# Projecting the values of a gated delta mixer once and convolving them on VectorE, a chunk ahead

## The reference, cut to what matters

```
q = x @ w_q;  k = x @ w_k;  v = x @ w_v                 # 1024, 1024 and 2048 channels
beta = sigmoid(x @ w_b) * 2
g = -exp(A_log) * softplus(x @ w_a + dt_bias)
q, k, v = silu(conv4(q)), silu(conv4(k)), silu(conv4(v)) # causal, depthwise, 4 taps in time
q, k = l2norm(q), l2norm(k)
for t:                                                   # per head, S is 64 x 128
    S = S * exp(g_t);  mem = k_t @ S
    S = S + k_t^T (v_t - mem) * b_t;  o_t = (q_t / 8) @ S
y = o * rsqrt(mean(o*o) + eps) * norm_w * silu(x @ w_g)
out = y @ w_out
```

## Time and profile before

| | us |
|---|---|
| median of 3 runs | 5771.28 |
| profiled execution, own time | 5775.05 |
| its span, first to last instruction | 5773.2 |
| TensorE busy | 5136.3 (89%) |
| VectorE busy | 3784.4 (66%) |
| ScalarE busy | 2786.2 (48%) |
| GpSimd busy | 2260.3 (39%) |
| stretch of the 32 chunks of the first mixer | 69 to about 2965 |

### The profile page before, as it was taken

How to read it: one execution, slowest core, us unless ns; L and a number is a source line. 1 busy time by engine, 2 the same in 40 slices (tenths; PEclk the granted TensorE clock), 3 DMA queues, 4 the chain that set the end, 5 groups by cost and what they waited for, 6 DMA issues and landing times. The chain is left out here.

```text
span 5773.2 us, 105253 instructions
## 1 busy us (share of the span) xinstructions
PE 5136.3 (89%) x36890; PEld 3594.2 (62%) x36890; DVE 3784.4 (66%) x8870; ACT 2786.2 (48%) x6575; POOL 2260.3 (39%) x1588
## 2 busy tenths in 40 slices
PE   5999999999899999999989989995578787998998
PEld 3776776767677677776766646652146675664665
DVE  5656656566565665656658848845699736875884
ACT  1444444444344444444438838844400113883882
POOL 2424334243232433424337717713422114762761
PEclk7999999999999999999989989997699757998998
DMA  3000000000000000000010000000000000000000
GB/s 110 5 7 7 4 7 5 5 7 4 9 4 7 7 4 7 5 5 7 4 32 1 0 27 1 0 7 0 0 8 1 1 1 28 0 18 10 0 0 15
DMA packets 170268, 53.55 MB, mean 9 GB/s; under 512 B 142225, under 2 KB 166161, under 8 KB 169233
## 3 DMA queue, kind: packets, MB, share of 16 engines
q1 hardware_dynamic: 168736, 49.54, 3.7%
q10 hardware_dynamic: 1392, 2.20, 0.1%
HBM read 41.21 MB, written 10.49 MB: 9 GB/s over the span
## 5 line engine op out<-in xcount | busy, mean ns | idle before, releaser
L342 PE MATMUL gd_ps<-gd_taps,gd_xwin 128*128 128x512 f32 x2048 | 907.3, 598 | 8.0 <-ACT gd_qT L528 8.0
L342 PEld LDWEIGHTS gd_ps<-gd_taps,gd_xwin 128*128 128x128 f32 x2048 | 382.7, 191 | 465.5 <-issue 446.0
L787 POOL TENSOR_TENSOR gd_o_rn<-gd_tmp,gd_mhalf 128x8 f32<-128x8 f32 x64 | 103.5, 1635 | 1193.6 <-DVE gd_tmp L706 1193.6
L551 ACT ACTIVATE gd_X<-gd_ps 128x512 f32<-128x512 f32 x512 | 268.2, 633 | 541.6 <-PE gd_ps L384 541.6
L1298 ACT ACTIVATE L_ffn_s<-L_ffn_s,L_ffn_nb,L_ffn_r 128x128 f32<-128x128 f32 x1024 | 419.4, 482 | 3.1
L683 DVE TENSOR_TENSOR gd_Z<-gd_ps,cst 128x256 f32<-128x256 f32 x384 | 163.0, 425 | 327.0 <-PE gd_ps L422 261.0
L1118 POOL TENSOR_TENSOR L_ffn_t<-L_ffn_t 128x512 f32<-128x512 f32 x128 | 190.3, 1487 | 394.3 <-DVE L_ffn_t L1339 394.3
L781 POOL TENSOR_TENSOR gd_gate<-gd_gate,gd_norm_w 128x2048 f32<-128x2048 f32 x32 | 145.0, 4531 | 483.4 <-ACT gd_gate L516 483.4
L384 PE MATMUL gd_ps<-cst,gd_gV 128*128 128x128 f32 x2048 | 264.9, 278 | 53.8 <-DMA gd_gV<-gd_inverses 29.5
L384 PEld LDWEIGHTS gd_ps<-cst,gd_gV 128*128 128x128 f32 x2048 | 225.8, 143 | 77.5 <-ACT gd_decay L546 74.8
L516 ACT ACTIVATE gd_v<-gd_ps 128x512 f32<-128x512 f32 x128 | 76.4, 597 | 406.2 <-PE gd_ps L342 406.2
(11 more groups left out here) (376 smaller groups left out, 13405.1 us busy)
## 6 DMA issues: line engine op xcount, KB each, us to landing
L_ffn_sb_rope<-in_rope SPq DMA_DIRECT2D x4, 2048.0 KB, 8.2
gd_tap_row<-in_L_attn_conv_v SPq DMA_DIRECT2D x2, 2048.0 KB, 7.1
gd_blocks<-gd_nA SPq DMA_DIRECT2D x256, 16.0 KB, 1.7
gd_Z<-gd_blocks SPq DMA_DIRECT2D x32, 128.0 KB, 2.0
gd_inverses<-gd_Z SPq DMA_DIRECT2D x32, 128.0 KB, 1.7
gd_gV<-gd_inverses SPq DMA_DIRECT2D x256, 16.0 KB, 1.9
L_ffn_sb_wqkv<-in_L_ffn_wqkv SPq DMA_DIRECT2D x4, 768.0 KB, 8.7
gd_tap_row<-in_L_attn_conv_q SPq DMA_DIRECT2D x1, 2048.0 KB, 15.4
```

The costliest lines, as they stand in the source:

```text
L342: ins = pe.matmul(ps[4 + i % 2][:], xwin[:, t:t + P] if i < 8 else xwin[:, PAD:PAD + P], taps[:, t, 512 * SLICE[i]:512 * (SLICE[i] + 1)] i ...
L551: act.activation(heads(X, gi).rearrange("p h x -> p (h x)"), ps[4 + gi][:], ACT.Copy).then_inc(x_s.sem, 1)
```

## The change

For v the four tap-scaled copies of the weights go away. w_v and its taps are loaded as they are. Per chunk TensorE multiplies each of the 16 blocks of 128 value channels once with the whole window of 131 columns (`plain_values`), with channels on the partitions and time along the columns; three blocks share a PSUM bank, so there are six steps, through banks 4 and 5. ScalarE copies them to `plain_v`. VectorE convolves (`convolve`): for each of the 16 blocks one tensor_scalar for the first tap and three scalar_tensor_tensor that add the other taps, each on a window shifted by one column, 64 operations per chunk. TensorE then turns each result back (`pe.transpose`, four per `project` 4 to 7), and ScalarE evicts with Silu as before.

The plain values and the convolution of chunk n+1 are done within `late` of chunk n: the matmuls behind gate slice 11 and ahead of k·S, the 16 first-tap operations ahead of the levels, and two of the other 48 behind each mask and each addition. `xwin_v` is a second window, filled by GpSimd at the head of `late`. For the first chunk of a batch the plain values come ahead of `early` and all 64 operations stand between `norms_and_decays` and `mid`; the last chunk of a batch has nothing ahead.

```diff
-        taps = sb("taps", [P, TAPS, QKV])
+        taps = sb("taps", [P, TAPS, 2 * H * DK])
+        w_v = sb("w_v", [P, H * DV])
+        taps_v = sb("taps_v", [P, H, TAPS])
...
-            conv_src = [W["conv_q"], W["conv_k"], W["conv_v"][0:1024], W["conv_v"][1024:2048]]
+            conv_src = [W["conv_q"], W["conv_k"]]
...
+                    act.dma_start(w_v[:], W["w_v"]).then_inc(weights_in, 16)
+                    act.dma_start(taps_v[:], W["conv_v"].rearrange("(m p) t -> p m t", p=P)).then_inc(weights_in, 16)
...
-                    for q in range(4):
-                        dve.wait_ge(taps_in[q % 2], 16 * (q // 2 + 1))
+                    for q in range(2):
+                        dve.wait_ge(taps_in[q], 16)
...
+                    elif i < 8:
+                        if i == 4:
+                            w(cv_s.now(n))
+                        for k in range(4):
+                            ins = pe.transpose(out[:, P * k:P * (k + 1)], conv_v[:, 4 * (i - 4) + k], ident)
...
+                def plain_values(n, i):
+                    if i == 0:
+                        w(win_v.now(n))
+                    if i >= 2:
+                        w(pv_out.now(n, i - 2))
+                    for j in range(min(VPER, H - VPER * i)):
+                        m = VPER * i + j
+                        ins = pe.matmul(ps[4 + i % 2][:, (PAD + P) * j:(PAD + P) * (j + 1)], w_v[:, DV * m:DV * (m + 1)], xwin_v[:], start=True, stop=True)
+                    ins.then_inc(pv_mm.sem, 1)
...
                     for i in range(5, 12):
                         project(n, i)
+                    if ahead:
+                        for i in range(VSTEPS):
+                            if i < 2:
+                                w(proj_out.now(n, 10 + i))
+                            plain_values(n + 1, i)
...
                         if g0 == 0:
-                            w(proj_out.now(n, 11))
+                            w(pv_out.now(n + 1) if ahead else proj_out.now(n, 11))
...
+                    for i in range(VSTEPS):
+                        plain_values(b * NC, i)
+                    w(pv_out.now(b * NC))
                     early(b * NC)
...
+                def convolve(n, first, count):
+                    for j in range(first, first + count):
+                        t, m = divmod(j, H)
+                        window, tap = plain_v[:, m, t:t + P], taps_v[:, m, t:t + 1]
+                        if t:
+                            w(cv_s.now(n, j - H))
+                            ins = dve.scalar_tensor_tensor(conv_v[:, m], window, tap, conv_v[:, m], ALU.mult, ALU.add)
+                        else:
+                            if m % VPER == 0:
+                                w(pv_out.now(n, m // VPER))
+                            ins = dve.tensor_scalar(conv_v[:, m], window, tap, None, ALU.mult)
+                        ins.then_inc(cv_s.sem, 1)
...
+                    if ahead:
+                        convolve(n + 1, 0, H)
...
                             dve.tensor_tensor(heads(Z, gi), ps[gi][:, 0:256].rearrange("p (h x) -> p h x", h=HG), mask, ALU.mult).then_inc(z_s.sem, 1)
+                            if ahead:
+                                convolve(n + 1, H + 16 * l + 2 * gi, 2)
...
+                            if ahead:
+                                convolve(n + 1, H + 16 * l + 8 + 2 * gi, 2)
...
                     norms_and_decays(b * NC)
+                    convolve(b * NC, 0, TAPS * H)
                     mid(b * NC)
```

More of the change, by code:

```diff
@@ L113 @@
 DECAY_FLOOR = -1.0e4
+VPER = 3
+VSTEPS = -(-H // VPER)
 def load_and_transpose(nc, A, cst, xT, sems):
@@ L206, in _ @@
                     dve.memset(mhalf[:], -0.5).then_inc(zeros, 1)
-                    dve.wait_ge(raw_in, 48)
-                    for q in range(4):
-                        dve.wait_ge(taps_in[q % 2], 16 * (q // 2 + 1))
+                    dve.wait_ge(raw_in, 32)
+                    for q in range(2):
+                        dve.wait_ge(taps_in[q], 16)
                         for t in range(TAPS):
@@ L253, in sig @@
             return Signal(sems("gd_" + name), per, primed)
-        win = sig("window", 1)
+        win, win_v = sig("window", 1), sig("window_v", 1)
+        pv_mm, pv_out, cv_s = sig("plain_v_mm", VSTEPS), sig("plain_v", VSTEPS), sig("conv_v", TAPS * H)
         ab_mm, ab_out = sig("ab_mm", 1), sig("ab_out", 1)
@@ L340, in project @@
                         w(t_out.now(n, i - 2))
[L341 to L344, removed]
-                    ins.then_inc(proj_mm.sem, 1)
+                    out = ps[4 + i % 2]
+                    if i < 4:
+                        for t in range(TAPS):
+                            ins = pe.matmul(out[:], xwin[:, t:t + P], taps[:, t, 512 * SLICE[i]:512 * (SLICE[i] + 1)],
+                                            start=(t == 0), stop=(t == TAPS - 1))
+                    elif i < 8:
[4 more added lines that the diff above has]
+                    else:
+                        ins = pe.matmul(out[:], xwin[:, PAD:PAD + P], w_g[:, 512 * (i - 8):512 * (i - 7)], start=True, stop=True)
+                    ins.then_inc(proj_mm.sem, 1)
+                def plain_values(n, i):
[7 more added lines that the diff above has]
+                    ins.then_inc(pv_mm.sem, 1)
                 def early(n):
@@ L516, in project, with plain_values @@
                     act.activation(dst, src, ACT.Silu).then_inc(proj_out.sem, 1)
+                def plain_values(n):
+                    for i in range(VSTEPS):
+                        w(pv_mm.now(n, i))
+                        m = min(VPER, H - VPER * i)
+                        act.activation(plain_v[:, VPER * i:VPER * i + m].rearrange("p m x -> p (m x)"), ps[4 + i % 2][:, 0:(PAD + P) * m],
+                                       ACT.Copy).then_inc(pv_out.sem, 1)
                 def early(n):
@@ L537, in mid, with late @@
                     copy_qk(n, 0)
-                def late(n):
+                def late(n, ahead):
                     for i in range(4, 12):
                         project(n, i)
+                    if ahead:
+                        w(cv_s.now(n))
+                        plain_values(n + 1)
                     for gi in range(G):
@@ L794, in _ @@
                         n = b * NC + c
+                        w(pv_mm.now(n))
+                        window_v(n + 1, b, c + 1)
                         late(n)
```

33 lines of the change are left out of this document (19 added, 14 removed).

## The result

| | before | after |
|---|---|---|
| median of the runs | 5772.8 us (5764.0 to 5775.0) | 6135.6 us (6125.0 to 6141.6) |
| the profiled execution, its span | 5775.05, 5773.2 | 6125.01, 6123.2 |
| granted TensorE clock, mean | 0.934 | 0.894 |

The changed kernel takes 1.063 times as long (95% interval 1.061 to 1.065). That is slower, as forecast, but 26 us beyond the upper end of the range of 5880 to 6110 and 96 us above the predicted 6040.

The account below looks back on a forecast made before the run. The chain from nA to the landed inverse, without TensorE, was taken as the bound. 30 chunks at +7.65 us (230), two last (7), starts +46 and set-up -13 gave +270: 6040 us predicted, range 5880 to 6110.

Parts of the forecast that it names:

- Part 1: TensorE between nA and the landed inverse: the 8.5 us saved per chunk become wait, except -0.75 us for q·S copies.
- Part 2: GpSimd's gate multiply, now earlier, stops VectorE's block inverse through the shared port: +4.4 us per chunk on the chain.
- The small reads of the earlier trace: GpSimd's 2.90 us power operation, reading 16 elements, let six chained VectorE operations pass undisturbed, 0.2 us each.
- Part 3: TensorE's longer idle before the turning of T drops its clock to 1.2 GHz: +1.7 us per chunk.
- The one case I priced it by: After a 5.23 us TensorE idle, 16 transposes took 3.98 us instead of 1.92; the clock was 1.00 in the stretch behind.
- Part 4: VectorE's convolution lengthens level 64: +2.3 us in each of 30 chunks; covered ahead of and in levels 16 and 32.
- Part 5: Batch starts and set-up: nA of a batch's first chunk 23 us later, twice, +46; set-up -13.
- PE busy less by about 240: A sign named in advance: TensorE's busy time falls by about 240 us while the mixer gets longer.
- (a): Rival: the port does not stop the inverse, since GpSimd waits or the gate is done before; 5900 us, chance 0.28.
- (b): Rival: the convolution lies on the path in full, 5.4 us for 2.3, with the port stop; 6135 us, chance 0.05.
- (c): Rival: same time, with inverse undisturbed, convolution hidden in TensorE's time and clock kept; 5780 us, chance 0.03.
- (d): Rival: faster, the inverse's landing follows TensorE's pace, so its 8.5 us per chunk come through; 5600 us, chance 0.04.

Follow-up runs that it names:

- b2: The kernel before with one tap of four for v and GpSimd's gate multiply made to wait for the block inverse's end; 5873 us, 1.018 times before.
- b1: The kernel before with one tap of four for v, 10.6 us less TensorE work per chunk and nothing added; 6008 us, 1.042 times before.
- a1: The changed kernel with GpSimd's gate multiply made to wait for the end of the block inverse; 5980 us, 1.037 times before.
- a2: The changed kernel with level 64's 16 convolution operations moved ahead of level 16; 6069 us, 1.051 times before.
- c2: c1 with k·S ahead of the next chunk's k projection and k scaled right behind level 64; 5728 us, 0.9925 times before.
- a4: The changed kernel with the edits of a1 and a2, and half the q·S products repeated three more times; 5918 us, 1.026 times before.
- c1: The changed kernel with the next chunk's k projection in TensorE's wait, convolution operations redistributed, gate multiply behind the levels; 5961 us, 1.033 times before.
- a3: The changed kernel with half the q·S products repeated ten more times to fill TensorE's wait; 6137 us, 1.064 times before.
- a5: a4 with seven repeats of half the q·S products in place of three; 5870 us, 1.018 times before.

## Why the prediction came out as it did

**Part 1 was right.** What TensorE saved became wait: 11.4 us per chunk, within the 7 to 12 named. That removing its work alone brings nothing, b2 shows: the chain is 21.42 us with 10.6 us less of it. The copies of q·S gave 1.14 us, not 0.75.

**Part 2 was right.** One operation of the inverse takes 4.57 us, and the chain went from 21.5 to 26.1 us where 26 was named; b1 against b2, and after against a1, give 4.2 to 4.3 for the meeting. The 0.3 us between the two starts in my schedule was 0.05 on average, between 1.2 us ahead of the inverse and 1.9 behind its beginning. The small reads of the earlier trace rows were no guide; the earlier trace rows were. The lock for a whole instruction, as the Trainium skill has it ("SBUF — State Buffer", "SBUF: two separate sides"), agrees here: the VectorE operation ended at 1218.71, GpSimd's at 1218.67.

**Part 3 failed in its size, and this is the step that put the time out of the range.** I took +1.7 us per chunk, "with ends of 0.8 and 3.4"; measured are 4.2, that is 134 us where 51 stood in the sum. The one case I priced it by the earlier trace rows had the clock back within 3.5 us, and I let the upper end be "twice as long a low stretch". In 22 of the 32 chunks of after that held: low for 2.8 to 5.3 us behind the wait. In the other 10 it lasted 19.1 to 19.8 us, through all of level 16, which then takes 16.3 to 16.6 us instead of 8.85. (The 11 chunks in the expectation of a1 are one too many.) A mechanism seen once had been given a range from that one case; a second sort of outcome was not in it. The rule of the Trainium skill on transposes that I weighed against the earlier trace rows ("TensorE: Matmul & The Clock Gate", "Part 4: PE-mode transpose") does not hold throughout here: in 8 chunks of after the clock rose 2.8 to 3.4 us behind the wait, when only transposes had run since it. In 14 it rose behind them, as the rule has it, and in the ten long ones 13 us of ordinary products did not raise it either.

**Part 4 was right in kind and a little low:** +2.87 us in level 64 for +2.3, 17 us in all; nothing in levels 16 and 32, as said, and a2 took exactly this term away.

**Part 5:** +28 for +33. Batch two's start is 23 us longer, as predicted. The nA of the first chunk came at 104.6, not 109, since the taps' row landed earlier: the fold of the taps starts at 32.77 where it was 37.78 in the earlier trace rows.

The misses add up: 83 (clock) + 17 (level 64) + 5 (chain) - 12 (copies) - 5 (starts) = 88 on the 6045 predicted for the profiled execution gives 6133; it took 6125. "PE busy less by about 240" was wrong by 156, for the most part for the same reason: the low clock doubles the durations of what runs in it, 8.6 us more of it per chunk, half of which is added time, 137 us.

Of the rivals, (a) is refuted by the operation of 4.57 us, and a1, which undoes it, gains 156 us where (a) stood 141 below the forecast; (b)'s 6135 was hit by number alone: the convolution cost 2.87 per chunk, not 5.4. (c) and (d) are out, since the landing never came earlier and the clock fell.

## What to carry to other kernels

Before TensorE's work is cut, look for what it waits for at the next meeting with another chain: if that wait is already there, even at 1 us, the cut is worth the copies behind it and no more, until work from behind the meeting is moved ahead of it, as in c2. An idle that this opens is not free on either side: it can drop the clock for what follows, and it lets an operation that was late (here GpSimd's multiply) slide onto the chain. When a mechanism is priced from a single instance in the trace, its range has to be wider than that instance.

## What the runs showed of the hardware that was not expected

- The low clock behind an idle has two lengths. In after, 22 chunks have it for 2.8 to 5.3 us behind the wait and 10 for 19.1 to 19.8 us, behind like idles and the same instructions. The idle's length does not tell them apart in these runs: idles of 11, 7 and 4.8 us (after, a1, a4) all give about 9 us per chunk on average. The moment at which the clock fell does: in the ten long ones it had fallen 7.54 to 8.26 us ahead of the first transposes, in the other 22 at most 7.49 or at least 8.34 us ahead. b1 divides as cleanly, with 11.06 to 11.52 us in its ten long ones and none of the other 22 in between. Why is not shown; no run moved that moment on purpose.
- An idle of 1.23 us is enough where it falls behind spaced transposes (four at a time, 0.4 us apart) and 64-column products (c1, in 30 chunks); of the 1 us idles at other places in before none lowered the clock, while some of 2.1 to 2.4 us did.
- A VectorE operation of 15 columns took 4.57 us instead of 0.2 beside a GpSimd multiply of 2048 columns. This happened in all 32 chunks of after: some operation of the inverse took 3.4 to 4.6 us.
- "issue" stalls of 3 to 4 us appear on TensorE in the kernels with the most matmuls per chunk (100 us in 55 stalls in a3, 28.8 in a5, none in a4), which before and after lack at that place. The DMA sections of the pages point at the fetching of instructions: the queue named so moved 339 packets in a3 and 140 in a5, against 83 in after and 84 in a4 (packets, MB, share; after, then a3).

```profile
q8 instruction: 83, 1.36, 0.1%
```
```profile
q8 instruction: 339, 5.55, 0.4%
```

In a3 all 44 of these stalls that are over 0.5 us long end 1.2 to 1.7 us behind the landing of such a packet. No run varied the length of the code alone, so this is a strong hint and not a proof.
